# A first axis made for two units at once, and the turn-back of a unit one block later, in the filter stage of a four-layer block

## The reference

```
a = pad(denumerator, 1 row and column in front, value 1)      # 16x16 channel pairs, 9x9 taps
b = pad(numerators[0], 1 row and column in front, value 0)
H_truncated = rfft2(b, s=(128, 128)) / rfft2(a, s=(128, 128))
h_truncated = irfft2(H_truncated, s=(128, 128))
H_full = h0 + rfft2(h_truncated, s=(256, 256))
y = irfft2(rfft2(x, s=(256, 256)) * H_full)[:128, :128]        # summed over the input channels
```

## Time and profile before

| | |
|---|---|
| median of 3 runs | 3544.68 us |
| the profiled execution, its span | 3553.3 us, 3551.5 us |
| mean granted TensorE clock over the span | 0.965 |
| the filter stage | from 0 to about 640 us of the span |
| busy in those 640 us: TensorE, VectorE, ScalarE, GpSimd | 577, 474, 381, 472 us |

### The profile page before, as it was taken

One profiled execution on the slowest core, in us unless ns is written; L12 is line 12 of the kernel. 1 busy time (PEld: TensorE's weight loads), 2 busy tenths in 40 slices (PEclk: granted clock), 3 DMA queues, 4 the chain that ended last, 5 costly groups with the idle time before them and its releaser, 6 DMA issues. The chain is left out here.

```text
span 3551.5 us, 84555 instructions
## 1 busy us (share of the span) xinstructions
PE 3241.2 (91%) x37272; PEld 2672.4 (75%) x37272; DVE 1579.5 (44%) x1926; ACT 1682.7 (47%) x1763; POOL 1250.4 (35%) x1018
## 2 busy tenths in 40 slices
PE   6999999579997699999899999999989978699996
PEld 5999998279997566666687776666678754399996
DVE  6888876311111443444765543434664454311111
ACT  3666665245553244444554534444554421365560
POOL 5888885055552102222540001222280000165550
PEclk9999999789999899999999999999999988899998
DMA  0333334787775521222133332121222342767765
GB/s 18 112 120 118 119 116 136 198 218 198 195 194 125 155 95 53 90 72 79 64 107 100 108 113 84 59 95 48 95 72 66 95 151 39 196 197 199 203 183 154
DMA packets 259187, 429.34 MB, mean 121 GB/s; under 512 B 27479, under 2 KB 105817, under 8 KB 257369
## 3 DMA queue, kind: packets, MB, share of 16 engines
q1 hardware_dynamic: 247050, 402.99, 39.1%
q10 hardware_dynamic: 11792, 21.12, 1.6%
HBM read 306.59 MB, written 114.29 MB: 119 GB/s over the span
## 5 line engine op out<-in xcount | busy, mean ns | idle before, releaser
L138 PE MATMUL m_bank<-xn,w 128*128 128x512 f32 x1536 | 618.1, 402 | 31.9 <-DVE m_store L1548 11.7
L139 PE MATMUL m_bank<-xn,w 128*128 128x512 f32 x1536 | 602.5, 392 | 0.0
L140 PE MATMUL m_bank<-xn,w 128*128 128x512 f32 x1536 | 602.3, 392 | 0.0
L757 PE MATMUL c_acc<-c_shifted,c_filt 128*32 128x192 f32 (+7 forms) x11264 | 457.8, 317 | 54.6 <-DVE c_filt L840 51.0
L757 PEld LDWEIGHTS c_acc<-c_shifted,c_filt 128*32 128x32 f32 x11264 | 444.2, 158 | 62.8 <-issue 60.3
L803 POOL TENSOR_TENSOR c_filt<-c_filt 64x1408 f32<-64x1408 f32 x64 | 258.4, 4038 | 607.2 <-DMA c_filt<-filters_dram 607.2
L129 ACT ACTIVATE w<-raw_weights 128x2048 fp32r<-128x2048 f32 x96 | 373.0, 3886 | 102.3 <-PE m_bank L140 101.9
L138 PEld LDWEIGHTS m_bank<-xn,w 128*128 128x128 f32 x1536 | 291.0, 189 | 173.0 <-issue 76.3
L133 DVE TENSOR_TENSOR w<-raw_weights,w 128x2048 fp32r<-128x2048 f32 x86 | 333.5, 3878 | 159.4 <-ACT w L129 159.4
L140 PEld LDWEIGHTS m_bank<-xn,w 128*128 128x128 f32 x1536 | 290.8, 189 | 62.8
L139 PEld LDWEIGHTS m_bank<-xn,w 128*128 128x128 f32 x1536 | 290.9, 189 | 59.7 <-issue 2.2
(11 more groups left out here) (180 smaller groups left out, 6801.9 us busy)
## 6 DMA issues: line engine op xcount, KB each, us to landing
c_shifted<-spectrum_dram SPq DMA_DIRECT2D x256, 270.0 KB, 3.9
filters_dram<-f_stage SPq DMA_DIRECT2D x128, 512.0 KB, 3.5
c_filt<-filters_dram SPq DMA_DIRECT2D x256, 256.0 KB, 4.9
raw_weights<-in_L_conv_Wq SPq DMA_DIRECT2D x16, 2048.0 KB, 8.6
raw_weights<-in_L_conv_Wk SPq DMA_DIRECT2D x16, 2048.0 KB, 8.6
raw_weights<-in_L_conv_Wv SPq DMA_DIRECT2D x16, 2048.0 KB, 8.6
m_qf<-in_L_conv_Wout SPq DMA_DIRECT2D x128, 256.0 KB, 3.8
spectrum_dram<-s_rows SPq DMA_DIRECT2D x128, 136.0 KB, 2.4
```

The lines of the kernel that those rows point to most:

```text
L138: pe.matmul(out, w[0], x[0], start=first, stop=False)
L139: pe.matmul(out, w[0], x[1], start=False, stop=False)
L140: return pe.matmul(out, w[1], x[0], start=False, stop=last)
L757: mm = nc.tensor.matmul(acc[k % 2][phase][32 * s:32 * s + 32, 0:B, LAGS * kb:HALF], filt[:, k, phase, :, :, 4 * kb + s].rearrange("p j c - ...
```

## The change

The first axis is now made for a pair of units: 17 products of the same 65x128 table with 128 columns of taps in place of twice 17 with 64 columns. The chunk of 17 products is cut in 5 parts (4, 4, 4, 4, 1). The parts of a pair are spread over two steps: three parts of the pair two units ahead in an odd step (blocks 5, 6, 7), two parts in the even step behind it (blocks 5 and 6). `rows` gets two copies. The tables move: the lag groups from blocks 1 to 3 to blocks 2 to 4, and the slots from blocks 4 to 8 to blocks 5 to 9, where block 9 is block 0 of the next step, right behind the first octet there. The wait for the spectrum moves from block 1 to block 2, and so behind the second octet of the next unit. The prologue becomes step -1 of the same loop. VectorE's code is the same, but it reads the changed `LAG_GROUPS`.

```diff
-    NB, SETS, CHUNKS, DEEP = 9, 5, 4, 3
-    CHUNK_AT = {4: 0, 5: 1, 6: 2, 8: 3}
-    LAG_GROUPS = {1: range(0, 3), 2: range(3, 6), 3: range(6, 8)}
-    SLOT_UNITS = {4: range(0, 3), 5: range(3, 6), 6: range(6, 9), 7: range(9, 12), 8: range(12, 16)}
+    NB, SETS, CHUNKS, DEEP = 9, 5, 5, 3
+    LAG_GROUPS = {2: range(0, 3), 3: range(3, 6), 4: range(6, 8)}
+    SLOT_UNITS = {5: range(0, 3), 6: range(3, 6), 7: range(6, 10), 8: range(10, 13), NB: range(13, 16)}
...
-        rows = sb("rows", [128, 17, 2, PAIRS])
+        rows = sb("rows", [128, 2, 17, 2, 2 * PAIRS])
...
+        def chunks_in(q):
+
+            pair, parts = ((q + 3) // 2, range(0, 3)) if q % 2 else (q // 2 + 1, range(3, CHUNKS))
+            return {5 + n: (pair, c) for n, c in enumerate(parts)} if pair < UNITS // 2 else {}
...
-        def first_axis(q, c, bank):
-
+        def first_axis(pair, c, bank):
+
+            taps = taps_ab[:, 2 * pair:2 * pair + 2].rearrange("k u a n -> k (u a n)")
             for m, b in enumerate(blocks_of(c)):
-                mm = nc.tensor.matmul(chunk(bank)[:, m], taps_q[:, b], taps_ab[:, q], start=True, stop=True)
+                mm = nc.tensor.matmul(mid(bank)[:, m], taps_q[:, b], taps, start=True, stop=True)
             mm.then_inc(chunk_ready, 1)
...
-                if blk == 1:
+            def turn_back(q, blk):
+
+                if blk == 2:
                     pe.wait_ge(spec_ready, q + 1)
...
+            for q in range(-1, UNITS):
+                if q == 0:
+                    pe.wait_ge(consts_in, 32)
+                    pe.wait_ge(respread_split, 2)
                 for blk in range(NB):
-                    if blk % 2 == 0:
+                    if blk % 2 == 0 and q + 1 < UNITS:
                         second_axis(q + 1, blk // 2)
-                    turn_back(q, k, blk, chunks, chunks_before)
...
+                    if blk == 0 and q > 0:
+                        turn_back(q - 1, NB)
+                    if q >= 0:
+                        turn_back(q, blk)
+                    chunk(q, blk)
+            turn_back(UNITS - 1, NB)
```

More of the change, by code:

```diff
@@ L196, in blocks_of, with chunks_before @@
             return range(4 * c, 4 * c + 4 if c < CHUNKS - 1 else 17)
+        def chunks_in(q):
+            pair, parts = ((q + 3) // 2, range(0, 3)) if q % 2 else (q // 2 + 1, range(3, CHUNKS))
+            return {5 + n: (pair, c) for n, c in enumerate(parts)} if pair < UNITS // 2 else {}
+        def chunks_before(q):
+            return min(CHUNKS * ((q + 3) // 2) + (0 if q % 2 else 3), CHUNKS * UNITS // 2)
         def turned_of(bank):
             return ring[bank][0:64, 0:128]
-        def chunk(bank):
-            return ring[bank][:].rearrange("p (m n) -> p m n", m=8)
         def mid(bank):
@@ L255, in _ @@
                 sp.wait_ge(stored[jp], 16 * PIECES * UNITS // 2)
[L257 removed]
+        def first_axis(pair, c, bank):
+            taps = taps_ab[:, 2 * pair:2 * pair + 2].rearrange("k u a n -> k (u a n)")
             for m, b in enumerate(blocks_of(c)):
[L260 removed]
+                mm = nc.tensor.matmul(mid(bank)[:, m], taps_q[:, b], taps, start=True, stop=True)
             mm.then_inc(chunk_ready, 1)
         def second_axis(q, octet):
[L265 removed]
+            pair, u = divmod(q, 2)
+            nc.tensor.wait_ge(rows_ready, pair * CHUNKS + octet + 1)
             if q or octet:
@@ L271, in second_axis @@
                         mm = nc.tensor.matmul(ab[:, 4 * r:4 * r + 4, part], taps_p[32 * r:32 * r + 32, part],
-                                              rows[32 * r:32 * r + 32, 4 * octet:4 * octet + 4], start=True, stop=True)
+                                              rows[32 * r:32 * r + 32, pair % 2, 4 * octet:4 * octet + 4, u], start=True, stop=True)
                 else:
-                    mm = nc.tensor.matmul(ab[:, 0, part], taps_p[0:32, part], rows[0:32, 16], start=True, stop=True)
+                    mm = nc.tensor.matmul(ab[:, 0, part], taps_p[0:32, part], rows[0:32, pair % 2, 16, u], start=True, stop=True)
             mm.then_inc(ab_ready, 1)
@@ L326, in _, with chunk @@
             pe.wait_ge(taps_in, 32)
-            def turn_back(q, k, blk, chunks, chunks_before):
-                if blk == 1:
+            def turn_back(q, blk):
+                if blk == 2:
                     pe.wait_ge(spec_ready, q + 1)
                 for g in LAG_GROUPS.get(blk, ()):
-                    to_lags(q, k, g, chunks_before)
+                    to_lags(q, q % 2, g)
                 for kb in SLOT_UNITS.get(blk, ()):
                     to_slots(q, kb)
-                if blk in CHUNK_AT and chunks:
-                    c = CHUNK_AT[blk]
-                    if c == 0:
+            def chunk(q, blk):
+                if blk in chunks_in(q):
+                    pair, c = chunks_in(q)[blk]
+                    if blk == 5 and q >= 0:
@@ L339, in turn_back @@
                         pe.wait_ge(lags_low, q * 8 + 8)
[L340 to L344, removed]
+                    pe.wait_ge(rows_ready, pair * CHUNKS + c)
+                    first_axis(pair, c, LAST)
+            for c in range(CHUNKS):
+                if c == 4:
+                    pe.wait_ge(rows_ready, 1)
+                first_axis(0, c, c % 4)
@@ L382, in split_den, with rows_out @@
                 nc.scalar.activation(sq[:, s, 0:f], of_ab(blk, slice(0, 2), 0), ACT.Square).then_inc(den_ready, 1)
-            def rows_out(q, c, bank):
+            def rows_out(pair, c, bank):
                 at = blocks_of(c)
-                act.wait_ge(chunk_ready, q * CHUNKS + c + 1)
-                nc.scalar.activation(rows[:, at[0]:at[-1] + 1].rearrange("p b a n -> p b (a n)"), chunk(bank)[:, 0:len(at)],
+                act.wait_ge(chunk_ready, pair * CHUNKS + c + 1)
+                nc.scalar.activation(rows[:, pair % 2, at[0]:at[-1] + 1].rearrange("p b u n -> p b (u n)"), mid(bank)[:, 0:len(at)],
                                      ACT.Copy).then_inc(rows_ready, 1)
@@ L407, in turn_back @@
                     slots_out(pair, jp, kb)
-            def step(pair, jp, chunks):
-                q = 2 * pair + jp
+            for c in range(CHUNKS):
+                rows_out(0, c, c % 4)
+            for q in range(-1, UNITS):
                 for blk in range(NB):
-                    if blk % 2 == 0:
+                    if q < 0 and blk == 1:
+                        act.wait_ge(consts_in, 32)
+                        split_high(nc.scalar, respread[:, 0], respread_raw[:]).then_inc(respread_split, 1)
+                    if blk % 2 == 0 and q + 1 < UNITS:
                         split_den(q + 1, blk)
                         split_den(q + 1, blk + 1)
[L415 to L437, removed]
+                    if blk == 0 and q > 0:
+                        turn_back((q - 1) // 2, (q - 1) % 2, NB)
+                    if q >= 0:
+                        turn_back(q // 2, q % 2, blk)
+                    if blk in chunks_in(q):
+                        rows_out(*chunks_in(q)[blk], LAST)
+            turn_back((UNITS - 1) // 2, 1, NB)
         @block.vector
```

16 lines of the change are left out of this document (4 added, 12 removed).

## The result

The changed kernel takes 3595.76 us (median of 4 runs, 3588.16 to 3628.55), the kernel before 3544.94 (4 runs): ratio 1.0141, 95% interval 1.0079 to 1.0203, 51 us slower. The direction was forecast, the size was not: 3557.7 had been said, at most 3574.

What follows compares the result with a forecast made beforehand. TensorE was taken as the bound; two new waits outweigh the first-axis gain: 14.4 - 0.5 - 0.4 + 1.1 + 0.3 - 1.8 = +13 us, so 3544.7 + 13 = 3557.7 us, range 3541 to 3574.

Steps and rivals of the forecast that it cites:

- First axis, 0.113 us per record: TensorE's first-axis products, filter stage: 128 columns take 0.113 us per record, 1.93 us per unit in place of 3.70.
- The bound of 0.22: Upper bound per first-axis record: twice the columns take twice the time, leaving no gain at all.
- New wait at the second octet, 1.7 us: TensorE waits 1.7 us per unit until VectorE's P1 is done; the second octet starts at 5.0.
- New wait at the first slot, 2.2 us: TensorE waits for VectorE's last two lag groups, 2.2 us where 0.41 stood; the first slot starts at 23.6.
- Sum for a step, 36.9 us: Filter-stage step: 23.6 + 11.2 + 1.93 + 0.15 = 36.9 us, against 35.72 on average before.
- The sum of +13 us without the clock: Whole kernel: twelve steps +14.4, the ends and prologue, and the tail together make +13 us, clock unchanged.
- rival C: The clock falls behind TensorE's two stops per unit (+25, 3582), or 128 columns cost more (3583); chance 8%.
- the stops of 1 us: Argument against a falling clock: TensorE's stops before never lowered it, and 2 us is nearer to these than 4.
- The sign that the prediction named for this: The prediction is wrong if the granted clock in the steady stretches is under 1.00.
- What bounds the kernel before: Filter stage: TensorE is the bound, busy 35.1 of 36 us; the other engines have some 6 us slack each.
- The gain of 1.77 us: Time saved per unit on TensorE by making the first axis for two units at once.
- The tail, -1.8: After the last spectrum: leftover slots fill most of TensorE's 4 us idle gap, avoiding a clock loss; -1.8 us.

Runs made afterwards that it cites:

- both stops filled: The changed kernel with idle matmuls added in the waits ahead of the second octet and the first slot; 3582.91 us against 3562.44 before, ratio 1.0072.
- the move alone: The kernel before with lags, slots and the spectrum wait one block later, first axis still for one unit; ratio 1.0255 to the kernel before.

## Why the prediction was right on the sign and wrong on the size

- *First axis, 0.113 us per record:* right, 0.113. The bound of 0.22 is out.
- *New wait at the second octet, 1.7 us:* right, 1.64.
- *New wait at the first slot, 2.2 us:* right; it starts at 23.61, its record shows 2.02 of idle time.
- *Sum for a step, 36.9 us:* right where the clock holds, 37.05.
- *The sum of +13 us without the clock:* right, 13.8 in the stage with both stops filled. So the sign was no luck.
- *The step that failed* is the clock. It stood in rival C, at 8% together with another case, and was put aside with "the stops of 1 us never did that, and 2 us is nearer to these". The price was taken as 1.75 us at least, 14 times, +25; the runs gave 36.3 and (659.83 - 628.08) 31.8 us. With the mechanism weighed as likely, 13 + 25 = 38 would have been most of the 51, and still too little. The row on which I judged it showed one stop of 4 us, and the "stops of 1 us" weren't in the rows at all: the earlier trace rows has one of 0.54 and one of 0.34 in the step, and only with the seams (0.61 and 0.41) do the two add up to 1. So the clock's holding was known for stops of half a microsecond and its fall for one of 4; two stops of about 2 us in one step lay between, where no row of before said anything. That is a case for a wide range, not for 8%. The sign that the prediction named for this, a clock under 1.00 in the steady stretches, was there (0.94). The Trainium skill, "TensorE: Matmul & The Clock Gate", section "HAM oscillation — how this bites in real kernels", tells of a loss of this kind, in a kernel that waits about 3 to 5 us for a DMA in each round and starts each round slow. Here it took less: the clock was at 0.50 behind the stop of 2.02 ahead of 121.94, though not in every step. The prediction cited the section and then didn't let it count.
- *What bounds the kernel before:* wrong without harm here. The gain of 1.77 us counted in full only because the move had taken the wait for the spectrum off the path; alone it was worth nothing (ratio 1.0021).
- *The tail, -1.8:* right. From the end of the last spectrum to the last slots it is 18.34 us before (595.92 to 614.26) and 16.67 in the changed kernel (647.67 to 664.34).

Open: whether two stops cost more clock than the sum of each alone, since the profiled executions and the medians differ on it, and why the same stops gave 0.90 with the move alone and 0.94 in the changed kernel.

## What to carry to other kernels

Before an engine's work is made shorter, close the loop: add up, from one release to the same release a step later, what stands between them on all engines. If the sum is the step, a busy engine inside it is not the bound. And price a new stop of TensorE twice, once by its length and once by the clock that it may cost; here stops of 3.7 us per step, 55 us in all, cost 32 to 36 us of clock on top in the profiled executions, more than twice the 13.8 that the change loses at full clock. A stop that can't be removed is a place for work that must be done anyway.

## What the runs showed of the hardware

- Stops of 1.64 and 2.02 us per step took the granted clock from 131 to 563 to 0.94 in the changed kernel and to 0.90 with the move alone; one of 3.6 us gave 0.91; one of 1.0 on average, with the first axis in the stops (12.3 us in 12 waits), 1.00; the 0.54 and 0.34 of the kernel before, 1.00 too. Either of the two alone left it at 0.99 in the profiled execution, but the 2.02 alone cost about 17 us by the medians. Behind a stop the clock was at 0.50 for some microseconds.
- The same program loses the clock in other steps in another execution.
- Idle multiplications in the stops made the kernel faster (ratio 1.0072 against 1.0145).
- A product of 128 weight columns costs 0.113 us per record with 128 columns and 0.111 with 64, at a granted clock of 1.00.
- In the first 60 us of both kernels the clock's column shows 1.00, but an octet takes 2.09 us there (at 27.12 and 33.14 before), as at 0.50 (126.82 in the changed kernel), and 1.15 in the steady steps. The pace of the records is the surer sign of the clock.
